# Four graph attention layers: the casts of the adjacency split between ScalarE and GpSimd

## The chip, the cores and the metric

The kernel runs on 1 core of one Trainium2 chip. The metric is the device time of one execution in microseconds (us), lower is better. The program has five instruction streams: TensorE (PE in the profile), VectorE (DVE), ScalarE (ACT), GpSimd (POOL) and SyncE (SP, which here only issues DMAs). They meet through semaphores.

## What is computed

Four pre-norm residual layers on a graph of N = 2048 nodes with 128 features: h = relu(layernorm(x)), x = x + attention_layer(h). Every layer uses the same adjacency matrix of 2048 x 2048 int32 zeros and ones. Cut to what matters:

```python
e = leaky_relu(s1[:, None] + s2[None, :], 0.2)      # scores from two vectors
att = softmax(where(adj > 0, e, NEG), axis=-1)      # 2048 x 2048
hp = elu(att @ Wh)                                  # layers 0, 2, 3; gelu in layer 1
# layer 0 does this for 8 heads, joins them and multiplies by W_out
```

The kernel factors exp(leaky_relu(s1 + s2)) into a row factor, a column factor and a maximum, so that an unnormalized probability is max(rho[i], t[j]) * adjT[j, i], with the column factor folded into V. The adjacency is needed as a bf16 factor of 0 or 1.

## The kernel before

**Tiling.** The transposed adjacency is cut into 32 tiles of 128 x 1024: tile n has half c = n // 16 of the columns (output rows) and block j = n % 16 of the neighbours. All stay in SBUF as bf16 (adjT) for the rest of the program. A head of layer 0 is two units of 16 steps, one for each half c; unit u = 2h + c. Step j of a unit: VectorE makes one tile of probs from rho, t_now and adjT (line 703), and TensorE multiplies it with V[j] in eight accumulating products that the trace shows as 16 matmuls (line 317). Between them lies a ring of 8 probs tiles, so VectorE is at most 8 steps ahead. In the first pass over the tiles (units 0 and 1, head 0) VectorE also waits for tile n of adjT to be cast.

**The loading of the adjacency.** SyncE issues 32 DMAs of 512 KB (line 181) into a staging buffer with STAGE = 5 slots, in order of n; DMA n waits for the cast of tile n - 5. ScalarE casts each tile with one activation, Sign (line 430), in groups that stand between its other duties: tiles 0 to 5 before the exponentials (line 549), then three after each of four groups of V (line 555), tiles 18 to 23 after copy_mean (line 558), and tiles 24 to 31 after it has copied waL (line 562). copy_mean waits for mean_rows, which TensorE does after step 7 of unit 0 (line 383); the copy of waL waits for later_vectors after step 13 (line 384).

**The row of rho.** rho is one row for each head, computed for all 8 heads in rho_rows. For unit 0 it is spread by TensorE. Otherwise GpSimd sends it through DRAM: for each half c it waits for the exponentials (rho_ready), stores the half of rho_rows to rho_dram (line 210), waits until that has landed, and, for c = 1, loads it spread over 128 partitions into rho (load_rho, line 205). Unit 1 waits for this load at its step 0 (line 789). The loads of the later heads follow in a loop (line 214), each after the unit that reads the old half.

**The end of a unit.** The work that follows a unit is done inside the next one (head0_asides, line 750): after step 7 VectorE computes the denominators (line 709), after step 8 it divides (line 725), for which ScalarE must first have made fill (lines 511 to 516, after the denominators), after step 10 it does the elu and a block transpose (lines 735 to 740); ScalarE then moves 16 blocks into hpT (line 529). TensorE takes hpT after its own step 10 of that unit (OUT_AT, line 341), and VectorE adds the result after its step 15.

ScalarE runs its stream in order, so fill_rows of unit 0 comes behind the cast of tile 31:

```python
            cast(24, 2 * NT)
            with act.Fori(0, H - 1) as h:
                finish(2 * h, 0)
```

Of the kernel before, what the change touches and what calls it, by code (L numbers as in the profile page):

```python
# [14 lines left out]
def gat_stack(nc, x, adj_t, w0, w0_t, a0, w_out, b_out, w1_t, w1, r1, w2, w2_t, av2, w3, w3_t, av3, out):  # L15
# [3 lines left out]
    ALU, ACT, AX = mybir.AluOpType, mybir.ActivationFunctionType, mybir.AxisListType  # L19
# [4 lines left out]
    NT = N // P  # L24
    CH = N // 2
# [5 lines left out]
    STAGE = 5  # L31
# [12 lines left out]
    with ctx:  # L44
        def sb(name, shape, dt=fp32):
            return ctx.enter_context(nc.sbuf_tensor(name, shape, dt))

        def sem(name):
            return ctx.enter_context(nc.semaphore(name))

        adjT = sb("adjT", [P, NT, N], bf16)
        stage = sb("stage", [P, STAGE, CH], i32)
# [55 lines left out]
        adj_in = [sem(f"adj_in{s}") for s in range(STAGE)]  # L108
        ident_zero = sem("ident_zero")
        ident_ready = sem("ident_ready")  # L110
        adj_ready = sem("adj_ready")
        wa_ready = sem("wa_ready")
        dve_step = sem("dve_step")
        wa_psum = sem("wa_psum")
# [46 lines left out]
        def group(c, k):  # L161

            return acc[:, c, k // PER_BANK, (k % PER_BANK) * VW:(k % PER_BANK) * VW + VW]

        def first_norm(n):

            return isinstance(n, int) and n == 0

        @block.sync
        def _(sp):  # L170
            for c in range(2):
                sp.dma_start(X[:, c * NK:(c + 1) * NK, :], x_v[:, c * NK:(c + 1) * NK, :]).then_inc(x_in[c], 16)
            sp.dma_start(W0t[:, :, :], w0_t.rearrange("h d f -> d h f")).then_inc(w0t_in, 16)
            sp.dma_start(a0_sb[:, :, :], a0).then_inc(w0t_in, 16)
            sp.dma_start(W0[:, :, :], w0.rearrange("h f d -> f h d")).then_inc(w0_in, 16)

            for n in range(2 * NT):
                c, j = n // NT, n % NT
                if n >= STAGE:
                    sp.wait_ge(adj_ready, n - STAGE + 1)  # L180
                sp.dma_start(stage[:, n % STAGE, :], adj_t[j * P:(j + 1) * P, c * CH:(c + 1) * CH]).then_inc(adj_in[n % STAGE], 16)
            sp.wait_ge(x_written, 10)
            sp.dma_start(out_v[:, 0:NK, :], X[:, 0:NK, :]).then_inc(out_done, 16)
            sp.wait_ge(x_written, 12)
            sp.dma_start(out_v[:, NK:NT, :], X[:, NK:NT, :]).then_inc(out_done, 16)
            sp.wait_ge(out_done, 32)

        @block.gpsimd
        def _(pool):
            nc.gpsimd.memset(ident[:, :], 0.0).then_inc(ident_zero, 1)  # L190
            pool.wait_ge(ident_zero, 1)
            nc.gpsimd.affine_select(out=ident[:, :], in_=ident[:, :], compare_op=ALU.not_equal, fill=1.0,  # L192
                                    base=0, pattern=[[-1, P]], channel_multiplier=1).then_inc(ident_ready, 1)
            for l, w in enumerate((w1_t, w2, w3)):
                pool.dma_start(WL[:, l, 0:D], w).then_inc(w_in, 16)
            for l, w in enumerate((w1, w2_t, w3_t)):
                pool.dma_start(WLt[:, l, :], w).then_inc(w_in, 16)
            for l, a in enumerate((r1, av2, av3)):
                pool.dma_start(aL_sb[:, l, :], a).then_inc(w_in, 16)
            pool.dma_start(bias_rep[:, :], b_out.rearrange("(o d) -> o d", o=1).to_broadcast([P, D])).then_inc(w_in, 16)  # L200
            pool.dma_start(Wout[:, :, :], w_out.rearrange("(h d) o -> d h o", h=H)).then_inc(w_in, 16)


            def load_rho(h, c):
                pool.dma_start(rho[:, c * CH:(c + 1) * CH],
                               rho_dram[bass.ds(h, 1), c * CH:(c + 1) * CH].to_broadcast([P, CH])).then_inc(rho_in[c], 16)

            for c in range(2):
                pool.wait_ge(rho_ready, 2 * c + 2)
                pool.dma_start(rho_dram[:, c * CH:(c + 1) * CH], rho_rows[:, c * CH:(c + 1) * CH]).then_inc(rho_stored, 16)  # L210
                pool.wait_ge(rho_stored, 16 * c + 16)
                if c == 1:
                    load_rho(0, c)
            with pool.Fori(0, H - 1) as h:
                for c in range(2):
                    pool.wait_ge(probs_ready, h * (2 * NT) + (c + 1) * NT)
                    load_rho(h + 1, c)

        @block.tensor
        def _(pe):  # L220
            def transpose_normed(n, c):

                for r in range(2 * c, 2 * c + 2):
                    pe.wait_ge(norm_act if r % 2 else norm_dve, 2 * n + c + 1)
                    for k in range(4):
                        last = nc.tensor.transpose(side[:, r % 2, k * P:(k + 1) * P],  # L226
                                                   xn[:, (r % 2) * 4 + k, :], ident[:, :])
                    last.then_inc(hT_psum, 1)
                if first_norm(n) or c == 1:
                    keep_warm(WARM_SHORT, idle_first if first_norm(n) else idle)  # L230
                pe.wait_ge(hT_ready, n * 4 + 2 * c + 2)
                if c == 0:
                    pe.wait_ge(wa_ready, n + 1)
# [190 lines left out]
        def _(act):  # L424
            def cast(n0, n1):

                for n in range(n0, n1):
                    c, j = n // NT, n % NT
                    act.wait_ge(adj_in[n % STAGE], 16 * (n // STAGE + 1))
                    nc.scalar.activation(adjT[:, j, c * CH:(c + 1) * CH], stage[:, n % STAGE, :], ACT.Sign).then_inc(adj_ready, 1)  # L430

            def relu_transposed(n, c):
                act.wait_ge(rstd_ready, n + 1 if first_norm(n) else 2 * n + c)
                for k in range(4, NK):
                    at = c * NK + k
                    last = nc.scalar.activation(xn[:, k, :], X[:, at, :], ACT.Identity, bias=nwt[:, 3, at:at + 1],  # L436
                                                scale=nwt[:, 0, at:at + 1])
                last.then_inc(norm_act, 1)
                for r in range(2 * c, 2 * c + 2):
                    act.wait_ge(hT_psum, n * 4 + r + 1)  # L440
                    nc.scalar.activation(hT[:, r * 512:(r + 1) * 512], side[:, r % 2, :], ACT.Relu,  # L441
                                         accum_out=hsum[:, r:r + 1]).then_inc(hT_ready, 1)
# [104 lines left out]
            relu_transposed(0, 0)  # L547
            relu_transposed(0, 1)
            cast(0, 6)
            factors(0, H)  # L550
            rho_exp(0, 0, H)
            act.wait_ge(tv_ready, 2)
            nc.scalar.activation(v_now[:, :], v_all[:, 0, :], ACT.Copy).then_inc(tv_ready, 1)
            act.wait_ge(tv_ready, 3)
            scale_v(0, lambda g: (cast(6 + 3 * g, 9 + 3 * g), g == 1 and rho_exp(0, 1, H)))
            copy_mean(1, H)
            take_mean(mean_w[:, 0:D], 1)
            cast(18, 24)
            act.wait_ge(waL_psum, 1)
            nc.scalar.activation(WL[:, 0:3, D], side[:, 0, 1:6:2], ACT.Copy)  # L560
# [43 lines left out]
        def _(dve):  # L604
# [181 lines left out]
            def rho_and_adj(h, c, blocks):  # L786
                def before(j):
                    if j == 0 and c == 1:
                        dve.wait_ge(rho_in[1], (h + 1) * 16)
                    elif j == 0 and not isinstance(h, int):  # L790
                        dve.wait_ge(rho_in[0], h * 16)
                    if blocks:
                        dve.wait_ge(adj_ready, c * NT + j + 1)
                return before

            def add_bias():
# [25 lines left out]
            for _, work in head0_asides(2 * H - 1, 1, store=False):  # L822
                work()
# [29 lines left out]
            with dve.Fori(0, 2) as l:  # L853
                base[0] = l * PER + outside
                n, u, f = l + 2, 2 * l + U2, 2 * l + 2 * H
# [50 lines left out]
```

## Time and profile before

| what | us |
|---|---|
| median of 3 runs (lowest to highest) | 807.01 (806.09 to 807.22) |
| the profiled execution | 807.67 |
| its span in the trace | 805.6 |
| TensorE busy | 775.1 (96%) |
| VectorE busy | 636.6 (79%) |
| ScalarE busy | 320.5 (40%) |
| GpSimd busy | 16.1 (2%) |
| casts of the adjacency on ScalarE, 32 | 31.7 |

The trace counts from the start of the span; the profiled execution has 2.1 us around it. The granted clock is the share of full speed that TensorE was given in a stretch.

### The profile page before, as it was taken

Reading aid. Unit: us, or ns where it says so; the run is one execution under the profiler, and the core shown is the slowest. Engines: PE = TensorE matmul, PEld = TensorE weight load, DVE = VectorE, ACT = ScalarE, POOL = GpSimd, SP = SyncE. Lnnn points to the kernel's source line nnn. Section 1 sums busy time; section 2 is a strip of 40 time slices with the busy share of each in tenths; the row PEclk is TensorE's granted clock in tenths of the full one; section 3 lists DMA queues with packets and bytes.
Section 4 is the critical chain, followed back from the end, with each engine's and each line's share of the span. In section 5 each row is a group of like instructions: output and inputs, shape, how many; then the busy total and the mean of one; then the engine's idle time right before and its main releaser. Section 6 shows DMA issues by size and latency. Waiting matters only on the chain. (4 is left out here: it accounts for less than half of the span.)

```text
span 805.6 us, 16634 instructions
## 1 busy us (share of the span) xinstructions
PE 775.1 (96%) x6666; PEld 755.5 (94%) x6666; DVE 636.6 (79%) x1084; ACT 320.5 (40%) x847; POOL 16.1 (2%) x34
## 2 busy tenths in 40 slices
PE   8999799999999999999999999999899989998995
PEld 8699799999999999999999999998799979987995
DVE  4595787877967978888788788796599569966994
ACT  2866443543345146144244354345420262135212
POOL 3000000000000000000000000000000000000000
PEclk8899999999999999999999999999999999999999
DMA  9687000000000000000000000000000000000000
GB/s 284 209 294 259 27 2 27 3 23 26 0 26 26 0 26 0 26 26 0 26 26 0 26 12 14 0 1 1 1 2 1 2 1 1 2 0 0 0 26 26
DMA packets 13708, 29.24 MB, mean 36 GB/s; under 512 B 1264, under 2 KB 7408, under 8 KB 13680
## 3 DMA queue, kind: packets, MB, share of 16 engines
q1 hardware_dynamic: 10992, 19.93, 7.5%
q0 software_dynamic: 2688, 8.92, 3.1%
q8 instruction: 20, 0.33, 0.2%
q14 instruction: 8, 0.07, 0.0%
HBM read 27.73 MB, written 1.11 MB: 36 GB/s over the span
## 5 line engine op out<-in xcount | busy, mean ns | idle before, releaser
L317 PE MATMUL acc<-V,probs 128*128 128x129 f32 x5632 | 639.0, 275 | 5.3 <-DVE probs L703 5.3
L317 PEld LDWEIGHTS acc<-V,probs 128*128 128x128 f32 x5632 | 634.0, 192 | 9.4 <-DVE probs L703 4.9
L703 DVE SCALAR_TENSOR_TENSOR probs<-rho,t_now,adjT 128x1024 f32<-128x1024 f32 x352 | 430.5, 1278 | 32.0 <-PE acc L317 26.2
L529 ACT ACTIVATE hpT<-rows 32x256 f32<-32x256 f32 x240 | 99.4, 414 | 76.2 <-DVE rows L740 73.5
L514 ACT ACTIVATE fill<-mean_now,empty 128x128 f32<-128x128 f32 x160 | 48.9, 394 | 102.4 <-DVE den L716 102.3
L748 DVE TENSOR_TENSOR X<-X,side 128x512 f32<-128x512 f32 x32 | 22.0, 688 | 61.5 <-PE side L341 61.5
L521 ACT ACTIVATE rows<-rows 128x512 f32<-128x512 f32 x44 | 27.7, 630 | 73.2 <-DVE rows L725 48.2
L725 DVE SCALAR_TENSOR_TENSOR rows<-acc,den,fill 128x128 f32<-128x128 f32 x160 | 43.9, 342 | 6.2 <-ACT fill L514 5.5
L463 ACT ACTIVATE V<-v_now 128x4 f32<-128x4 f32 x32 | 6.7, 209 | 85.8 <-PE side L262 85.8
L341 PE MATMUL side<-Wout,hpT 128*128 (+1 forms) x256 | 33.0, 284 | 4.5 <-ACT hpT L529 4.2
L436 ACT ACTIVATE xn<-X,nwt 128x128 f32<-128x128 f32 x36 | 14.8, 483 | 56.3 <-DVE nwt L640 56.3
L465 ACT ACTIVATE V<-side,v_now 128x128 f32<-128x128 f32 x128 | 36.1, 365 | 0.0
L341 PEld LDWEIGHTS side<-Wout,hpT 128*128 128x128 f32 x256 | 31.4, 200 | 4.9 <-issue 4.4
L262 PE MATMUL side<-W,hT 128*128 (+1 forms) x256 | 34.7, 279 | 0.0
L282 PEld LDWEIGHTS acc<-ident 128*128 128x128 f32 x236 | 31.1, 215 | 3.5 <-ACT V L479 1.9
L282 PE MATMUL acc<-ident 128*128 128x128 f32 x236 | 32.3, 300 | 1.8 <-POOL ident L192 1.6
L262 PEld LDWEIGHTS side<-W,hT 128*128 128x128 f32 x256 | 31.8, 195 | 2.4 <-issue 2.4
L430 ACT ACTIVATE adjT<-stage 128x1024 bf16<-128x1024 int32 x32 | 31.7, 1058 | 4.7 <-DMA stage<-in_adj_t_dram 4.7
L441 ACT ACTIVATE hT<-side 128x512 f32<-128x512 f32 x18 | 10.6, 594 | 26.7 <-PE side L226 26.6
L653 DVE COPY den<-acc 128x6 f32<-128x6 f32 x22 | 3.5, 157 | 21.9 <-PE acc L317 21.9
L736 DVE SCALAR_TENSOR_TENSOR rows<-rows 128x1024 f32<-128x1024 f32 x16 | 19.6, 1225 | 0.6
L740 DVE STREAM_TRANSPOSE rows<-rows 128x1024 f32<-128x1024 f32 x15 | 18.7, 1246 | 0.5
(107 smaller groups left out, 277.8 us busy)
## 6 DMA issues: line engine op xcount, KB each, us to landing
stage<-in_adj_t_dram SPq DMA_DIRECT2D x32, 512.0 KB, 6.6
rho<-rho_dram POOLq DMA_DIRECT2D x15, 512.0 KB, 3.9
X<-in_x_dram SPq DMA_DIRECT2D x2, 512.0 KB, 4.4
out_dram<-X SPq DMA_DIRECT2D x2, 512.0 KB, 3.2
W0t<-in_W_t_dram SPq DMA_DIRECT2D x1, 512.0 KB, 7.1
W<-in_L_gnn_W_heads_dram SPq DMA_DIRECT2D x1, 512.0 KB, 7.7
Wout<-in_L_gnn_W_out_dram POOLq DMA_DIRECT2D x1, 512.0 KB, 10.4
WL<-in_L_gnn_W_dram POOLq DMA_DIRECT2D x2, 64.0 KB, 5.9
```

What stands on the lines that cost most here:

```text
L262: last = nc.tensor.matmul(side[:, g % 2, k * D:(k + 1) * D], hT[:, j * P:(j + 1) * P], w, start=True, stop=True)
L282: nc.tensor.matmul(where, ident[:, :], ident[:, :], start=True, stop=True)
L317: last = nc.tensor.matmul(group(c, k), probs[:, j % RING, k * P:(k + 1) * P], V[:, j, :], start=(j == 0 and k % PER_BANK == 0), stop=(j == ...
L341: last = nc.tensor.matmul(side[:, b, k * D:(k + 1) * D], hpT[:, 4 * b + k, :], w, start=True, stop=True)
L430: nc.scalar.activation(adjT[:, j, c * CH:(c + 1) * CH], stage[:, n % STAGE, :], ACT.Sign).then_inc(adj_ready, 1)
L465: last = nc.scalar.activation(V[:, 4 * g + k, 0:D], side[:, g % 2, k * D:(k + 1) * D], ACT.Copy, scale=v_now[:, 4 * g + k:4 * g + k + 1])
L514: ins = nc.scalar.activation(fill[:, k, :], mean_now[:, :], ACT.Copy, scale=empty[:, c, k:k + 1])
L521: nc.scalar.activation(rows[:, 1, 4 * b:4 * b + 4, :], rows[:, 0, 4 * b:4 * b + 4, :], func).then_inc(act_ready, 1)
L529: last = nc.scalar.activation(hpT[b:b + Q, :, a:a + Q], rows[a:a + Q, 1, :, b:b + Q], ACT.Copy)
L703: nc.vector.scalar_tensor_tensor(probs[:, j % RING, :], rho[:, c * CH:(c + 1) * CH], t_now[:, j:j + 1], adjT[:, j, c * CH:(c + 1) * CH], A ...
L725: ins = nc.vector.scalar_tensor_tensor(rows[:, 0, k, :], group(c, k)[:, 0:D], den[:, 3, k:k + 1], fill[:, k, :], ALU.mult, ALU.add)
L748: nc.vector.tensor_tensor(at, at, side[:, b, :].rearrange("p (k d) -> p k d", k=4), ALU.add).then_inc(x_added, 1)
```

## The change

Tiles with n % 3 == 2 (2, 5, 8, ..., 29: ten of the 32) are cast by GpSimd with a comparison, is_gt against 0, and the other 22 by ScalarE as before. The one semaphore that counted casts becomes two, and a helper, wait_adj, turns the number of a tile into the semaphore and the count to wait for; SyncE and VectorE use it. In GpSimd's stream tiles 2, 5, 8 and 11 stand ahead of the store of the first half of rho_rows, tiles 14, 17, 20 and 23 ahead of the store of the second half (and so ahead of load_rho for unit 1), and tiles 26 and 29 behind that load and ahead of the loop.

```diff
-        adj_ready = sem("adj_ready")
+        adj_act = sem("adj_act")
+        adj_pool = sem("adj_pool")
...
+        def on_pool(n):
+
+            return n % 3 == 2
+
+        def wait_adj(engine, n):
+
+            before = sum(on_pool(i) for i in range(n + 1))
+            engine.wait_ge(adj_pool if on_pool(n) else adj_act, before if on_pool(n) else n + 1 - before)
...
                 if n >= STAGE:
-                    sp.wait_ge(adj_ready, n - STAGE + 1)
+                    wait_adj(sp, n - STAGE)
...
+            def cast(n0, n1):
+
+                for n in range(n0, n1):
+                    c, j = n // NT, n % NT
+                    if on_pool(n):
+                        pool.wait_ge(adj_in[n % STAGE], 16 * (n // STAGE + 1))
+                        nc.gpsimd.tensor_scalar(adjT[:, j, c * CH:(c + 1) * CH], stage[:, n % STAGE, :], 0, None,
+                                                ALU.is_gt).then_inc(adj_pool, 1)
+
             for c in range(2):
+                cast(12 * c, 12 * c + 12)
                 pool.wait_ge(rho_ready, 2 * c + 2)
                 pool.dma_start(rho_dram[:, c * CH:(c + 1) * CH], rho_rows[:, c * CH:(c + 1) * CH]).then_inc(rho_stored, 16)
                 pool.wait_ge(rho_stored, 16 * c + 16)
                 if c == 1:
                     load_rho(0, c)
+            cast(24, 2 * NT)
...
-                    act.wait_ge(adj_in[n % STAGE], 16 * (n // STAGE + 1))
-                    nc.scalar.activation(adjT[:, j, c * CH:(c + 1) * CH], stage[:, n % STAGE, :], ACT.Sign).then_inc(adj_ready, 1)
+                    if not on_pool(n):
+                        act.wait_ge(adj_in[n % STAGE], 16 * (n // STAGE + 1))
+                        nc.scalar.activation(adjT[:, j, c * CH:(c + 1) * CH], stage[:, n % STAGE, :], ACT.Sign).then_inc(adj_act, 1)
...
                     if blocks:
-                        dve.wait_ge(adj_ready, c * NT + j + 1)
+                        wait_adj(dve, c * NT + j)
```

## Rows read from the trace of the kernel before

**Rows 1.** The page, part 1: busy us (share of the span) and instructions.

```profile
PE 775.1 (96%) x6666; PEld 755.5 (94%) x6666; DVE 636.6 (79%) x1084; ACT 320.5 (40%) x847; POOL 16.1 (2%) x34
```

**Rows 2.** Waits of TensorE, 60 to 560 us: total, times, longest.

```profile
PE side L341 <- ACT hpT L529: 4.2, 1, 4.2
PE acc L246 <- ACT hT L441: 0.9, 1, 0.9
```

**Rows 3.** Timeline of ScalarE: start, us, line, operation, tiles, count, [idle before, releaser].

```profile
56.46 1.09 ACT L502 ACTIVATE mean_w<-side 128x512 f32<-128x512 f32 x2 [4.79 <-PE side L302]
57.92 4.84 ACT L430 ACTIVATE adjT<-stage 128x1024 bf16<-128x1024 int32 x5
...
67.87 4.84 ACT L430 ACTIVATE adjT<-stage 128x1024 bf16<-128x1024 int32 x5
...
76.84 1.06 ACT L430 ACTIVATE adjT<-stage 128x1024 bf16<-128x1024 int32 x1 [2.61 <-DMA stage<-in_adj_t_dram]
78.08 1.06 ACT L430 ACTIVATE adjT<-stage 128x1024 bf16<-128x1024 int32 x1 [0.19 <-DMA stage<-in_adj_t_dram]
79.04 2.43 ACT L514 ACTIVATE fill<-mean_now,empty 128x128 f32<-128x128 f32 x8
...
88.19 6.80 ACT L529 ACTIVATE hpT<-rows 32x256 f32<-32x256 f32 x16 [4.90 <-DVE rows L740]
```

**Rows 4.** Timeline of VectorE: steps of units 0 and 1, denominators, division.

```profile
49.61 8.46 DVE L703 SCALAR_TENSOR_TENSOR probs<-rho,t_now,adjT 128x1024 f32<-128x1024 f32 x7
58.25 1.28 DVE L703 SCALAR_TENSOR_TENSOR probs<-rho,t_now,adjT 128x1024 f32<-128x1024 f32 x1 [0.18 <-PE acc L317]
60.04 1.28 DVE L703 SCALAR_TENSOR_TENSOR probs<-rho,t_now,adjT 128x1024 f32<-128x1024 f32 x1 [0.50 <-PE acc L317]
...
72.70 0.15 DVE L653 COPY den<-acc 128x6 f32<-128x6 f32 x1
...
73.23 0.20 DVE L716 RECIPROCAL den<-den 128x8 f32<-128x8 f32 x1
...
80.34 2.29 DVE L725 SCALAR_TENSOR_TENSOR rows<-acc,den,fill 128x128 f32<-128x128 f32 x8 [5.50 <-ACT fill L514]
...
86.91 1.25 DVE L740 STREAM_TRANSPOSE rows<-rows 128x1024 f32<-128x1024 f32 x1
```

**Rows 5.** Timeline of TensorE: the first output projection.

```profile
95.24 3.61 PE L341 MATMUL side<-Wout,hpT 128*128 x16 [4.20 <-ACT hpT L529]
```

**Rows 6.** Busy us of each engine by stretch, TensorE's granted clock, DMA share, GB/s.

```profile
34.00:58.00 24.00, 23.60 (x175) 20.72 (x174) 23.48 (x23) 17.01 (x33) 1.08 (x2) 0.94 0.92 318
95.20:98.80 3.60, 3.56 (x17) 3.56 (x18) 0.69 (x1) 0.04 (x1) 0.10 (x1) 0.53 0.44 146
```

**Rows 7.** Timeline of SyncE's queue, 58 to 62 us.

```profile
59.01 3.17 SPq L181 DMA_DIRECT2D stage<-in_adj_t_dram  x4
```

**Rows 8.** Timeline of GpSimd: its two elementwise instructions, then rho's store and load.

```profile
0.87 0.20 POOL L190 MEMSET ident<- 128x128 f32 x1 [0.29 <-POOLq L896]
1.30 0.28 POOL L192 TENSOR_SCALAR_AFFINE_SELECT ident<-ident 128x128 f32<-128x128 f32 x1 [0.23 <-POOL ident L190]
...
42.23 0.51 POOL L210 DMA_DIRECT2D rho_dram<-rho_rows  x1 [9.46 <-ACT rho_rows L456]
47.45 0.57 POOL L205 DMA_DIRECT2D rho<-rho_dram  x1 [4.70 <-DMA rho_dram<-rho_rows]
```

**Rows 9.** DMA issues at 24.6, 59.0, 47.4, 58.8 and 94.8 us: size, us to landing.

```profile
stage<-in_adj_t_dram SPq DMA_DIRECT2D x1, 512.0 KB, 3.6
...
stage<-in_adj_t_dram SPq DMA_DIRECT2D x1, 512.0 KB, 4.9
...
rho<-rho_dram POOLq DMA_DIRECT2D x1, 512.0 KB, 9.1
...
rho<-rho_dram POOLq DMA_DIRECT2D x1, 512.0 KB, 5.0
...
rho<-rho_dram POOLq DMA_DIRECT2D x1, 512.0 KB, 4.0
```

## The prediction

> **What bounds the kernel now.** The page's busy shares come first: TensorE is busy for 775.1 us of a span of 805.6 [rows 1]. ScalarE, which the change relieves, is busy for 40%, so fewer casts are worth something only where TensorE waits for ScalarE. So I read TensorE's waits next, over the stretch that holds the casts and the seven heads after them. From 60 to 560 us it waits twice for ScalarE: 4.2 us for hpT, and 0.9 us in the next layer [rows 2]. The 4.2 us end at 95.24 [rows 5], and the weights matter: everything after that runs on TensorE without a gap to the next layer, so whatever moves 95.24 moves the end by the same amount. The matmuls behind that wait run at a granted clock of 0.53, about the lower level of 1.2 GHz against 2.4 [rows 6]; the 16 matmuls take 3.61 us [rows 5].
>
> The timelines of ScalarE and VectorE show where the 4.2 us come from. Unit 0's denominators are there at 73.23 + 0.20 = 73.43 [rows 4], but ScalarE casts to the end of tile 31, 78.08 + 1.06, and begins fill at 79.04; it had stood 2.61 us for the DMA of tile 30 [rows 3]. VectorE waits 5.50 us for fill [rows 4]. From the start of fill the chain is fixed: 79.04, division at 80.34, steps 9 and 10, elu, transpose to 86.91 + 1.25, the 16 block moves to 88.19 + 6.80 = 94.99 [rows 3, 4]. That is **15.95 us from fill to hpT**, and TensorE goes on 0.25 later. So the number that decides is the time at which fill of unit 0 can start.
>
> **What the change removes.** Ten casts of 0.97 us (4.84 us for five [rows 3]) leave ScalarE, 9.7 us of busy time. Up to 58 us TensorE is busy 23.60 us of 24 [rows 6] and VectorE has made all 16 probs tiles of unit 0 at 49.61 + 8.46 = 58.07 while TensorE ends that unit more than 13 us later (it paces the ring at 60.04 - 58.25 = 1.79 us a step [rows 4], and 95.24 less the wait of 4.20 less 11 steps of unit 1 is 71.35). So earlier casts there are worth nothing. At the end ScalarE gets tiles 24 to 31 done a little sooner, but it is not short of ScalarE time there: it waits for DMAs 30 and 31 [rows 3], and these wait for the casts of 25 and 26, which cannot start before 67.87. By itself this would let fill start between 77 and 79 instead of 79.04, a gain of 0 to 2 us.
>
> **What the change moves.** The program of GpSimd now has four casts ahead of each store of rho. The first store loses its place from 32 us to about 40, with no one behind it before the load for unit 2, which is asked for after 58 us. The second is another matter. Before, the store went at 42.23 and the load at 47.45 [rows 8], and the load landed 9.1 us later [rows 9], at 56.5, just ahead of VectorE's step 0 of unit 1 at 58.25 [rows 4]. Now both stand behind the cast of tile 23. The earliest time for that follows from the code and rows: slot 23 % 5 is free when tile 18 is cast; tile 18 remains ScalarE's, and stands behind copy_mean, which waits for TensorE's step 7. So it is cast from 57.92 [rows 3], and the DMA of tile 23 goes at 59.01 [rows 7], after the change as before it. No engine that the change relieves is on this path. From there:
>
> - DMA of tile 23: 3.6 us with little beside it, 4.9 beside a load of rho [rows 9]. That load of rho now comes later, so I take 3.8: 62.8.
> - The cast on GpSimd. No row shows one. GpSimd's nearest instruction that reads a tile is the affine select, 0.28 us for 128 columns; eight times that is 2.3. Its memset of 128 columns took 0.20 [rows 8]; ScalarE's cast 0.97 stands for the low end, as I have no reason to think GpSimd quicker. I take 1.6, between them: 64.4. A gain below nothing is excluded, since a cast takes some time and none stood there.
> - Store to load: 47.45 - 42.23 = 5.2 us [rows 8], at a busy DMA, as here: 69.7 with a hand-over.
> - The load: 4.0 us alone, 5.0 beside two stage loads, 9.1 behind a row of them [rows 9]. At 69.7 the DMAs of tiles 29 and 30 have just been issued (casts of 24 and 25 from 67.87), so I take 5.3: **rho for unit 1 at 75.0**.
>
> VectorE stands at step 0 of unit 1 from 58.07 to 75.0; behind that wait are queued all probs tiles of unit 1, the denominators, the division and the elu. TensorE runs dry at 71.35 and starts again about 1.3 us after rho, at 76.3, an idle time of 4.9 us. That stall itself has cover: the 11 steps before hpT then end at 76.3 + 19.7 = 96.0, or 97.8 with a slow start of 1.8, and TensorE has to wait for hpT anyway (below: to 101.6).
>
> What counts is the chain on VectorE. Steps 0 to 7 of unit 1 had been made long before 72.70; now they come after 75.0, at 8.46 / 7 = 1.21 us each [rows 4], so 9.7 us, then the denominators, 73.43 - 72.70 = 0.7 us. Fill starts at 75.0 + 10.4 = 85.4 instead of 79.04, 6.4 us later; ScalarE has been free since about 78. The 15.95 us follow as before, hpT is there at 101.4, and TensorE resumes 6.4 us later, at 101.6. Its wait there is 3.8 to 5.6 us, near the 4.2 of before, so I leave the slow clock behind it as it is: 3.61 us for 16 matmuls against 1.79 for 16 at full clock, 1.8 us in both.
>
> The other waits are small. Tiles 26 and 29 are cast behind the load of rho; DMA 31 waits for tile 26 and lands at about 77, needed by VectorE not before 90. The load for unit 2 goes after the cast of tile 29, about 76, and is needed at 106. The two counters cost no instruction on a busy engine.
>
> **Sum.** 6.4 us on the profiled execution's 807.67 is 814.1; the median of the runs is 0.66 below that execution, so I forecast 813.5. Low end of the mechanism: 59.01 + 3.6 + 1.0 + 5.1 + 4.0 = 72.7, fill 4.1 us later, 811.1. If TensorE kept the full clock behind its wait, 1.8 less, 809.3. High end: 59.01 + 4.9 + 2.3 + 5.3 + 9.1 = 80.6, 12 us later, 819.
>
> **Rivals.** *Rho is no later than unit 1 needs it (the other side).* The point from which this decides: fill starts earlier than 79.04 only when rho lands before 79.04 - 10.4 = 68.6. Then what is left is ScalarE's gain of 0 to 2 us, 805 to 807. For it speaks that the load had 1.7 us of room before, and that TensorE has 13 us of probs in its ring when VectorE ends unit 0; against it, that the three fixed pieces alone (DMA 3.6, store 5.1, load 4.0, from 59.01) give 71.7 with a cast that costs nothing. It needs one of them at half of what any row shows.
>
> *GpSimd and VectorE hold each other up.* In 34 to 58 us VectorE is busy 23.48 us of 24 [rows 6], nearly all in line 703, which reads rho and adjT. No row shows GpSimd reading a tile at that time. If GpSimd gets through only when VectorE stands still, tile 11 is cast when VectorE itself waits for it, about 52 us; store 1 behind it takes 5.2, tile 14 is cast to 60, tile 17 to 62, DMA 19 waits for tile 14 and DMA 23 stands behind four others (five of 512 KB at 318 GB/s, 8 us): landing at 69 to 70, rho at 82, fill 13 us later, 820. If they only take turns, each cast costs VectorE up to 2.3 us where it is 8 tiles ahead, which is free, and tile 23 is cast while VectorE stands: the main forecast. The Trainium skill ("SBUF — State Buffer", section "Who interferes with whom") states that a VectorE instruction with two SBUF inputs and a GpSimd instruction that reads SBUF exclude each other and the second to issue waits for the whole of the first; by it 813.5 stands if the turns alternate and about 820 if VectorE always comes first, and no row of before shows which.
>
> The same notes ("GPSIMD Engine Reference", section "Performance versus the Vector engine") give 1.8 cycles per element at 1.2 GHz for a tight loop of one input, so an estimate of 1.5 us for 1024 columns; the sum by it would be 0.1 us lower.
>
> *A cast on GpSimd is much dearer than any row suggests*, say 4 us for a comparison with two conversions. Tiles 11, 14, 17, 20 still keep up (about 16 us apart in all, over 39 to 59), and the forecast moves by 2.4 to 816.
>
> **Chances.** Main chain with the bounds above 0.76; mutual hold-up 0.09; dear cast 0.08; rho in time after all 0.07, of which 0.04 faster and 0.03 within 0.2%. A difference of 0.2%, 1.6 us, is about what a measurement of this kernel can tell from none. Faster 0.04, same 0.03, slower 0.93. The range from 810.0 to 819.5 leaves out the rival on the other side, the worst of the hold-up and the tail of both ends.
>
> **What would show it.** In the trace of the changed kernel: the DMA of tile 23 still at about 59.0; GpSimd's cast of tile 23 at 62 to 64 and its length; store and load of rho 5.2 us apart; a new wait of VectorE's line 703 for rho of some 17 us, ending near 75; TensorE idle from 71 to 76; fill near 85.4, released by the denominators and no longer by a cast; TensorE's output projection at about 101.6 instead of 95.24, and from there all work shifted alike. The prediction is wrong if the load of rho lands before 68.6, if fill does not follow the load by 10.4 us, or if VectorE waits for a tile cast by GpSimd in unit 0.

## The result and the profile after

The changed kernel takes 816.2 us (median of 4 runs, 815.76 to 821.01) against 806.55 us (median of 4, 805.96 to 807.22). The ratio is 1.0133, with a 95% interval of 1.0094 to 1.0172: slower, by 8 to 14 us. The two profiled executions are 816.23 and 807.67 us, 8.56 apart, and their spans 814.2 and 805.6, 8.6 apart. TensorE's busy time is the same (775.0 us, before 775.1); what is new is idle time between 60 and 104 us. ScalarE's share fell from 40% to 38%, GpSimd's rose from 2% to 6%.

First GpSimd's timeline of the changed kernel (start, us, line, operation, tiles, count, [idle before, releaser]): the casts of tiles 14 and 17, of 20, of 23, then the store of rho's second half and the load for unit 1.

```profile
48.98 7.57 POOL L224 TENSOR_SCALAR adjT<-stage 128x1024 bf16<-128x1024 int32 x2 [4.93 <-DMA rho_dram<-rho_rows]
60.32 2.99 POOL L224 TENSOR_SCALAR adjT<-stage 128x1024 bf16<-128x1024 int32 x1 [3.77 <-DMA stage<-in_adj_t_dram]
64.95 2.77 POOL L224 TENSOR_SCALAR adjT<-stage 128x1024 bf16<-128x1024 int32 x1 [1.64 <-DMA stage<-in_adj_t_dram]
67.66 0.60 POOL L230 DMA_DIRECT2D rho_dram<-rho_rows  x1
72.98 0.56 POOL L215 DMA_DIRECT2D rho<-rho_dram  x1 [4.72 <-DMA rho_dram<-rho_rows]
```

Where the load went out at 47.45 before [rows 8], it goes at 72.98. The DMAs on that path: SyncE's issue of tile 23, its time to landing, and that of rho's load.

```profile
59.27 0.33 SPq L191 DMA_DIRECT2D stage<-in_adj_t_dram  x1
...
stage<-in_adj_t_dram SPq DMA_DIRECT2D x1, 512.0 KB, 5.6
...
rho<-rho_dram POOLq DMA_DIRECT2D x1, 512.0 KB, 4.2
```

VectorE's timeline answers [rows 4]: the last seven steps of unit 0, the first eight of unit 1 behind a wait of 16.67 us for rho, the denominators.

```profile
50.79 9.90 DVE L725 SCALAR_TENSOR_TENSOR probs<-rho,t_now,adjT 128x1024 f32<-128x1024 f32 x7
77.35 9.65 DVE L725 SCALAR_TENSOR_TENSOR probs<-rho,t_now,adjT 128x1024 f32<-128x1024 f32 x8 [16.67 <-DMA rho<-rho_dram]
86.92 0.16 DVE L675 COPY den<-acc 128x6 f32<-128x6 f32 x1
...
87.46 0.20 DVE L738 RECIPROCAL den<-den 128x8 f32<-128x8 f32 x1
```

ScalarE's timeline answers [rows 3]: it has finished tile 31 at 81.16 and then waits 6.54 us for the denominators, so fill has changed its releaser, from the casts to VectorE.

```profile
58.18 2.01 ACT L452 ACTIVATE adjT<-stage 128x1024 bf16<-128x1024 int32 x2
...
80.10 1.06 ACT L452 ACTIVATE adjT<-stage 128x1024 bf16<-128x1024 int32 x1 [3.51 <-DMA stage<-in_adj_t_dram]
87.70 2.45 ACT L536 ACTIVATE fill<-mean_now,empty 128x128 f32<-128x128 f32 x8 [6.54 <-DVE den L738]
...
96.87 6.80 ACT L551 ACTIVATE hpT<-rows 32x256 f32<-32x256 f32 x16 [4.90 <-DVE rows L762]
```

TensorE's timeline: it runs dry for 7.04 us, then has 11 steps, then waits 3.25 us for hpT. It resumes at 103.92, where it resumed at 95.24 before [rows 5]: 8.68 later, which is the whole difference.

```profile
67.83 3.82 PE L338 MATMUL acc<-V,probs 128*128 128x129 f32 x32
78.69 21.98 PE L338 MATMUL acc<-V,probs 128*128 128x129 f32 x176 [7.04 <-DVE probs L725]
103.92 3.46 PE L362 MATMUL side<-Wout,hpT 128*128 x16 [3.25 <-ACT hpT L551]
```

### The profile page after: what moved, and what is told of

Same layout as the page of the kernel before. It is cut to its first block and busy times, and to the rows that moved or that the text cites. A ratio compares the mean times of both kernels' runs of the same rounds, so it can differ in the third digit from the quotient of the medians.

```text
span 814.2 us, 16634 instructions
## 1 busy us (share of the span) xinstructions
PE 775.0 (95%) x6666; PEld 755.6 (93%) x6666; DVE 639.4 (79%) x1084; ACT 311.6 (38%) x837; POOL 47.2 (6%) x44
## 5 line engine op out<-in xcount | busy, mean ns | idle before, releaser
L725 DVE SCALAR_TENSOR_TENSOR probs<-rho,t_now,adjT 128x1024 f32<-128x1024 f32 x352 | 432.2, 1285 | 44.2 <-PE acc L338 22.2
L362 PE MATMUL side<-Wout,hpT 128*128 (+1 forms) x256 | 32.8, 284 | 3.5 <-ACT hpT L551 3.2
L224 POOL TENSOR_SCALAR adjT<-stage 128x1024 bf16<-128x1024 int32 x10 | 31.1, 3119 | 33.5 <-DMA stage<-in_adj_t_dram 28.5
L215 POOL DMA_DIRECT2D rho<-rho_dram x15 | 8.1, 537 | 408.5 <-DVE probs L725 403.7
L452 ACT ACTIVATE adjT<-stage 128x1024 bf16<-128x1024 int32 x22 | 22.4, 1058 | 9.8 <-DMA stage<-in_adj_t_dram 9.7
```

The lines of the kernel that those rows point to most:

```text
L224: nc.gpsimd.tensor_scalar(adjT[:, j, c * CH:(c + 1) * CH], stage[:, n % STAGE, :], 0, None, ALU.is_gt).then_inc(adj_pool, 1)
L362: last = nc.tensor.matmul(side[:, b, k * D:(k + 1) * D], hpT[:, 4 * b + k, :], w, start=True, stop=True)
L725: nc.vector.scalar_tensor_tensor(probs[:, j % RING, :], rho[:, c * CH:(c + 1) * CH], t_now[:, j:j + 1], adjT[:, j, c * CH:(c + 1) * CH], A ...
```

## The experiments

The start of the program, to unit 0, varies by several us from run to run (single runs of the kernel before lay between 804.4 and 811.4 in the experiments). From TensorE's return, the start of the first output projection, to the end of the span it is 710.2 to 711.6 us in the traces of this table, and 708.9 in e5 and e7, so differences of about 1 us arise behind it too. So each trace is also read from a fixed event in it: the start of copy_mean on ScalarE. "Behind" is the span less that start; the last column is its difference from before.

| kernel | copy_mean | fill | span | behind | against before |
|---|---|---|---|---|---|
| before | 56.46 | 79.04 | 805.6 | 749.1 | |
| changed | 56.72 | 87.70 | 814.2 | 757.5 | +8.3 |
| e1_place_only | 54.48 | 86.88 | 813.6 | 759.1 | +10.0 |
| e11_place_only_hold | 54.44 | 86.80 | 814.3 | 759.9 | +10.7 |
| e3_tile23_act | 59.22 | 85.84 | 813.3 | 754.1 | +4.9 |
| e4_tiles20_23_act | 56.52 | 83.16 | 810.2 | 753.7 | +4.5 |
| e8_place_early | 57.13 | 78.72 | 805.4 | 748.3 | -0.9 |
| e2_load_first | 61.37 | 82.95 | 809.4 | 748.0 | -1.1 |
| e6_load_first_act26 | 57.17 | 78.88 | 806.7 | 749.5 | +0.4 |
| e5_before_act26 | 55.68 | 75.32 | 800.4 | 744.7 | -4.4 |
| e7_before_act28 | 55.11 | 74.50 | 799.6 | 744.5 | -4.7 |

### e1_place_only: the place of rho's store and load alone

On the kernel before; no cast on GpSimd.

```diff
             for c in range(2):
+                if c == 1:
+                    pool.wait_ge(adj_ready, 24)
                 pool.wait_ge(rho_ready, 2 * c + 2)
```

> The kernel before with all 32 casts on ScalarE; GpSimd only waits for the cast of tile 23 before it stores the second half of rho_rows. My theory (the place of rho's store and load is the whole cost): ScalarE ends tile 23 at about 65.0, load issued at 70.3 (5.3 us after the store, as in the changed kernel), VectorE's step 0 of unit 1 at 74.7, fill 10.35 us later at 85.0 instead of 79.04, so 6.0 us slower than before. The rest of the change's 8.7 us would be the longer cast on GpSimd and the later landing of tile 23. Rival (the slow casts on GpSimd, or their contention with VectorE, are the cost): within 0.5 us of before.

Measured: 817.51 us against 807.7, ratio 1.014 (1.0092 to 1.0187). The place alone costs as much as the whole change, which settles the cause; the size was missed by 4 us (6.0 expected, 9.8 by the medians, 10.0 behind copy_mean). GpSimd's and VectorE's timelines of this kernel:

```profile
62.29 0.51 POOL L212 DMA_DIRECT2D rho_dram<-rho_rows  x1 [30.89 <-ACT adjT L432]
68.35 0.57 POOL L205 DMA_DIRECT2D rho<-rho_dram  x1 [5.54 <-DMA rho_dram<-rho_rows]
...
76.54 9.66 DVE L705 SCALAR_TENSOR_TENSOR probs<-rho,t_now,adjT 128x1024 f32<-128x1024 f32 x8 [20.32 <-DMA rho<-rho_dram]
```

Store to load took 6.1 us (5.3 in the changed kernel), load to use 8.2 (4.4 there). So without GpSimd's casts the store went out earlier, and store and load were slower.

### e11_place_only_hold: what made that load slow

On e1_place_only.

```diff
+            pool.wait_ge(adj_ready, 2 * NT)
             with pool.Fori(0, H - 1) as h:
```

> The run with only the place of rho's store and load moved, in which the load for unit 1 took 8.1 us to be used where the changed kernel took 4.4; here the load for unit 2 is held back until all 32 tiles are cast, so that it does not follow 0.8 us behind the load for unit 1. Theory A (the second load delayed the first): step 0 of unit 1 comes 4.5 to 5.5 us after the load's issue, 3 us earlier, and the time falls to about 6.5 to 7.5 us above before. Theory B (the stage DMAs in flight delayed it): still about 8 us from issue to use, and about 9.5 us above before.

Measured: 816.96 against 807.82, ratio 1.0116 (1.008 to 1.0152). GpSimd's and VectorE's timelines:

```profile
68.56 0.57 POOL L205 DMA_DIRECT2D rho<-rho_dram  x1 [5.80 <-DMA rho_dram<-rho_rows]
...
76.46 9.66 DVE L706 SCALAR_TENSOR_TENSOR probs<-rho,t_now,adjT 128x1024 f32<-128x1024 f32 x8 [20.28 <-DMA rho<-rho_dram]
```

Still 7.9 us from issue to use: theory A falls. What is left is the stage DMAs beside it. The stretch from the load's issue to its use, first here, then in the changed kernel, where it took 4.4 (columns: us, busy PE, PEld, DVE, ACT, POOL, granted clock, DMA share, GB/s):

```profile
68.56:76.40 7.84, 0.80 (x8) 0.61 (x6) 0.00 (x0) 3.92 (x5) 0.57 (x1) 0.84 0.85 274
72.98:77.30 4.32, 0.00 (x0) 0.00 (x0) 0.00 (x0) 2.11 (x2) 4.29 (x3) 0.87 0.60 231
```

In e4_tiles20_23_act the share is 1.00 and the load takes 7.8 us. So a busier DMA goes with a slower load, but the stage DMAs were not switched off by themselves: that they are the cause is not shown.

### e3_tile23_act and e4_tiles20_23_act: how far the store must move

On the changed kernel; the second has `and n not in (20, 23)`.

```diff
-            return n % 3 == 2
+            return n % 3 == 2 and n != 23
```

> The changed kernel with tile 23 given back to ScalarE, GpSimd's other nine stay. My theory: the store follows the cast of tile 20, which ended at 63.3 in the changed kernel, instead of tile 23's at 67.7; load issued at 68.6, VectorE's step 0 at 73.0, fill at 83.4: 4.4 us less than the changed kernel, 4.3 us more than before. Rival: if the cost were the casts themselves, one of ten gives back 0.9 us.

Measured: 813.35 against 807.7, ratio 1.0069 (1.0045 to 1.0093). GpSimd, VectorE and TensorE:

```profile
62.45 0.60 POOL L230 DMA_DIRECT2D rho_dram<-rho_rows  x1
67.70 0.56 POOL L215 DMA_DIRECT2D rho<-rho_dram  x1 [4.65 <-DMA rho_dram<-rho_rows]
...
74.72 10.43 DVE L725 SCALAR_TENSOR_TENSOR probs<-rho,t_now,adjT 128x1024 f32<-128x1024 f32 x8 [11.67 <-DMA rho<-rho_dram]
...
102.06 3.78 PE L362 MATMUL side<-Wout,hpT 128*128 x16 [4.44 <-ACT hpT L551]
```

From copy_mean to TensorE's return is 42.8 us, against 38.8 before and 47.2 in the changed kernel: one cast of ten, moved off the path of rho, gives back half, as expected, and not the tenth of the loss (0.9 us) that the rival gives. That it gives back just the 4.4 us forecast is partly luck. The store came 7.7 us earlier against copy_mean than in the changed kernel (copy_mean itself was 2.5 us later), and 3.4 us of that was lost again: the load took 7.0 us to its use instead of 4.4, and the eight steps 10.43 instead of 9.65.

> The changed kernel with tiles 20 and 23 given back to ScalarE. My theory: the store follows the cast of tile 17 at 56.6, load issued at 61.9, rho there at 66.3, which is before the 68.6 from which it decides: fill is bound by ScalarE's last casts at 77 to 79, so -2 to 0 us against before, though VectorE still waits some 7 us for rho. Rival (any wait of VectorE for rho costs its own length): 7 us slower than before; rival (the casts cost): 7 us slower as well.

Measured: 810.8 against 807.7, ratio 1.0034 (1.0014 to 1.0054): slower by 3 us where no loss was expected. GpSimd, VectorE and ScalarE:

```profile
56.30 0.60 POOL L230 DMA_DIRECT2D rho_dram<-rho_rows  x1
63.24 0.56 POOL L215 DMA_DIRECT2D rho<-rho_dram  x1 [6.35 <-DMA rho_dram<-rho_rows]
71.21 2.77 POOL L224 TENSOR_SCALAR adjT<-stage 128x1024 bf16<-128x1024 int32 x1 [7.41 <-DMA stage<-in_adj_t_dram]
75.06 3.28 POOL L224 TENSOR_SCALAR adjT<-stage 128x1024 bf16<-128x1024 int32 x1 [1.08 <-DMA stage<-in_adj_t_dram]
...
71.17 11.30 DVE L725 SCALAR_TENSOR_TENSOR probs<-rho,t_now,adjT 128x1024 f32<-128x1024 f32 x8 [10.69 <-DMA rho<-rho_dram]
...
83.16 2.45 ACT L536 ACTIVATE fill<-mean_now,empty 128x128 f32<-128x128 f32 x8 [4.29 <-DVE den L738]
```

The mechanism holds and two durations did not: store to load 6.9 us, load to use 7.9, so rho came at 71.2 and not at 66.3, 2.6 behind the point of 68.6; and VectorE's eight steps took 11.30 us instead of 9.7, since GpSimd's casts of tiles 26 and 29 fell beside them. 2.6 + 1.6 = 4.2 is fill's delay (83.16 against 79.04: 4.1). The rival of 7 us is out as well: 10.7 us of waiting for rho cost 4.

### e8_place_early: a wait for rho that lands in time

On the kernel before, as e1_place_only, with `pool.wait_ge(adj_ready, 16)`.

> The kernel before with the store of rho's second half held only until the cast of tile 15 (ScalarE ends it at about 51.7). Theory (only a load that lands after the point of 68.6 costs anything): store 52, load 57.3 to 58.5, landed at 62 to 66; VectorE waits 3 to 8 us for rho at step 0 of unit 1, TensorE does not run dry, and the time is that of before within 0.5 us. Rival (each us that VectorE waits for rho costs one): 3 to 8 us slower.

Measured: 807.52 against 806.9, ratio 1.0004 (0.9987 to 1.0021). A wait of VectorE, and TensorE's return:

```profile
DVE probs L705 <- DMA rho<-rho_dram: 2.6, 1, 2.6
...
94.92 3.06 PE L343 MATMUL side<-Wout,hpT 128*128 x16 [3.21 <-ACT hpT L531]
```

Rho's load was issued at 56.27 and VectorE began unit 1 at 61.3. VectorE waits 2.6 us, a little less than expected, TensorE does not run dry, and the time is that of before. So it is the point, not the wait, that decides.

### e2_load_first: all of the change but the place

On the changed kernel.

```diff
+            cast(0, 12)
             for c in range(2):
-                cast(12 * c, 12 * c + 12)
                 pool.wait_ge(rho_ready, 2 * c + 2)
                 pool.dma_start(rho_dram[...], rho_rows[...]).then_inc(rho_stored, 16)
-                pool.wait_ge(rho_stored, 16 * c + 16)
-                if c == 1:
-                    load_rho(0, c)
-            cast(24, 2 * NT)
+            pool.wait_ge(rho_stored, 32)
+            load_rho(0, 1)
+            cast(12, 2 * NT)
```

> The changed kernel with all ten casts on GpSimd, but both stores of rho_rows and the load for unit 1 stand behind tile 11 and ahead of tile 14. My theory: load issued at about 49.5, landed before 58.7, no wait of VectorE for rho; fill is again bound by ScalarE's last casts, which wait for DMAs 30 and 31, at 77.5 to 79.5, so -1.5 to +0.5 us against before. Rival (GpSimd's casts of 2.8 us and up are too slow for the staging buffer, or hold VectorE up): still 4 us or more slower than before, with VectorE or ScalarE waiting for tiles.

Measured: 808.53 against 807.7, ratio 1.0014 (0.9994 to 1.0034). GpSimd's load, ScalarE's fill, TensorE's return:

```profile
50.82 0.56 POOL L215 DMA_DIRECT2D rho<-rho_dram  x1 [3.43 <-DMA rho_dram<-rho_rows]
...
82.95 2.43 ACT L535 ACTIVATE fill<-mean_now,empty 128x128 f32<-128x128 f32 x8
...
99.17 3.43 PE L361 MATMUL side<-Wout,hpT 128*128 x16 [3.22 <-ACT hpT L550]
```

With ten casts on GpSimd and rho early, the loss is gone, and hardly anything is gained: fill is 21.6 us behind copy_mean (22.6 before), right behind ScalarE's last cast, as before. The start of the program took longer in this trace (copy_mean at 61.37); more on it below.

### e5_before_act26, e7_before_act28, e6_load_first_act26: what the casts were really bound by

e5 on the kernel before (e7 with 28 in place of 26; e6 is e5's edit on e2_load_first).

```diff
-            cast(18, 24)
+            cast(18, 26)
             act.wait_ge(waL_psum, 1)
...
-            cast(24, 2 * NT)
+            cast(26, 2 * NT)
```

> The kernel before with ScalarE's casts of tiles 24 and 25 moved ahead of the copy of waL, where it stood idle for 2.7 us; nothing on GpSimd. Theory (the 4.2 us wait of TensorE for hpT comes from casts that wait for DMAs 30 and 31, and these for the casts of 25 and 26): DMAs 29 and 30 go about 2 us earlier, fill starts at 76 to 77.5 instead of 79.04, 1.5 to 3 us faster than before. Rival (the DMA rate bounds the last tiles whatever the order): within 0.5 us of before.

Measured: 803.22 against 806.9, ratio 0.9957 (0.9934 to 0.9979). ScalarE's cast of tile 24 and fill; TensorE's return, and the stretch behind it (us, busy PE, PEld, DVE, ACT, POOL, granted clock, DMA share, GB/s):

```profile
65.13 1.06 ACT L430 ACTIVATE adjT<-stage 128x1024 bf16<-128x1024 int32 x1 [1.75 <-DMA stage<-in_adj_t_dram]
...
75.32 2.43 ACT L514 ACTIVATE fill<-mean_now,empty 128x128 f32<-128x128 f32 x8
...
91.53 2.05 PE L341 MATMUL side<-Wout,hpT 128*128 x16 [1.27 <-ACT hpT L529]
...
91.50:93.60 2.10, 2.07 (x18) 2.08 (x19) 0.69 (x1) 0.02 (x1) 0.09 (x1) 1.00 0.54 209
```

By the medians 3.7 us (the interval gives 1.7 to 5.3), more than expected, for two reasons: fill comes 2.9 us nearer to copy_mean, and behind the wait, now 1.27 us instead of 4.20, the clock is granted in full (1.00, against 0.53 [rows 6]), so the 16 matmuls take 2.05 us instead of 3.61 [rows 5].

> As the run with tiles 24 and 25 moved ahead, but with 24 to 27: the copy of waL comes at about 69, still ahead of unit 1 on TensorE at 71.4. Theory: DMA 31 goes 1 to 2 us earlier too; fill starts at 75 to 76.5, 3 to 4 us faster than before, and up to 6 if TensorE no longer waits and keeps its clock. Risk: if tile 27 lands late, the copy of waL is late and TensorE waits ahead of unit 1. Rival (DMA rate): within 0.5 us of before.

Measured: 802.94 against 806.9, ratio 0.9945 (0.9923 to 0.9967), not apart from e5. ScalarE and TensorE:

```profile
74.50 2.43 ACT L514 ACTIVATE fill<-mean_now,empty 128x128 f32<-128x128 f32 x8
...
90.70 2.05 PE L341 MATMUL side<-Wout,hpT 128*128 x16 [0.89 <-ACT hpT L529]
```

Only 0.89 us of the wait is left. This is the lowest median of all, with every cast on ScalarE.

> GpSimd casts its ten tiles, rho's stores and load stand ahead of tile 14, and ScalarE casts tiles 24 and 25 ahead of waL. Theory: DMAs 29 to 31 are now tied to GpSimd's casts of 23 and 26, each 2.8 to 3.9 us; fill relative to copy_mean no better than with the casts on ScalarE alone: 0 to 2.5 us faster than before, and behind the same order without GpSimd. If GpSimd's casts helped, it would be the faster of the two.

Measured: 807.71 against 806.9, ratio 1.0006 (0.9987 to 1.0025). GpSimd's cast of tile 26, and fill:

```profile
70.75 3.51 POOL L224 TENSOR_SCALAR adjT<-stage 128x1024 bf16<-128x1024 int32 x1 [3.63 <-DMA stage<-in_adj_t_dram]
...
78.88 2.43 ACT L535 ACTIVATE fill<-mean_now,empty 128x128 f32<-128x128 f32 x8
```

The gain of e5 is lost when GpSimd casts its share: tile 26 is done at 74.3, and DMA 31 waits for it. In e5 ScalarE had it done at 69.1. Of these 5.2 us, 1.5 come from the later start of this trace (copy_mean at 57.17, in e5 55.68).

### e9_gpsimd_reads and e10_gpsimd_writes: do the two engines hold each other up

On the kernel before, behind the load of rho for unit 1; e10 has `nc.gpsimd.memset(dum_in[:, :], 0)` in the loop. The scratch tiles, their semaphore and a first memset of dum_in at the start of GpSimd's program come with it and are not shown.

```diff
+            for k in range(8):
+                pool.wait_ge(dum, k + 1)
+                nc.gpsimd.tensor_scalar(dum_out[:, :], dum_in[:, :], 0, None, ALU.is_gt).then_inc(dum, 1)
             with pool.Fori(0, H - 1) as h:
```

> The kernel before with eight casts of a scratch tile (128 x 1024, int32 to bf16, the instruction of the change) on GpSimd behind the load of rho for unit 1, at 48 to 80 us, that nobody waits for. Theory (GpSimd's reads and VectorE's line 703 exclude each other in turns): a cast takes 3.6 to 3.9 us beside VectorE against 2.8 alone, and a step of line 703 that meets one takes longer than 1.21 us, 7 steps 9.3 to 9.9 instead of 8.5; no time lost, as VectorE is ahead there. Rival (no exclusion; the long casts have another reason): steps at 1.21 us as in the kernel before.

> The same with eight memsets of 128 x 1024 in place of the casts: GpSimd writes and reads nothing. Theory (it is GpSimd's read that collides with VectorE's two operands): steps of line 703 at 1.21 us, the memsets equally long beside VectorE and alone. Rival (any work of GpSimd collides): steps lengthened as with the casts.

One run of each: 806.23 and 803.06 us, beside one of 804.47 for before, which says nothing on time. GpSimd's eight instructions and VectorE's steps beside them, first e9_gpsimd_reads:

```profile
46.24 26.01 POOL L220 TENSOR_SCALAR dum_out<-dum_in 128x1024 bf16<-128x1024 int32 x8
...
47.46 24.14 DVE L710 SCALAR_TENSOR_TENSOR probs<-rho,t_now,adjT 128x1024 f32<-128x1024 f32 x15
```

and e10_gpsimd_writes:

```profile
44.50 8.04 POOL L220 MEMSET dum_in<- 128x1024 int32 x8
...
45.45 9.79 DVE L710 SCALAR_TENSOR_TENSOR probs<-rho,t_now,adjT 128x1024 f32<-128x1024 f32 x8
```

Beside the casts a step takes 24.14 / 15 = 1.61 us and a cast 3.25; beside the memsets a step takes 1.22, as alone, and a memset 1.0. So GpSimd's writes alone do not lengthen the steps, and the read is what is left; the cast also converts and compares, which no run separates from it. The steps were lengthened more than expected, the casts less (median 3.09 us of one, the rest of the 3.25 is the hand-over between two).

## Why the prediction was right, and where its terms were off

The forecast of 813.5 us was in the right direction and for the right reason; the measured 816.2 lies in the range. Point by point:

- *What bounds the kernel:* held. TensorE's return from hpT moved by 8.68 us and the span by 8.6. From fill to hpT it is 103.67 - 87.70 = 15.97 us, forecast 15.95; from rho to fill 87.70 - 77.35 = 10.35, forecast 10.4.
- *Tile 18 stays behind copy_mean:* held; the DMA of tile 23 went at 59.27 (59.01 before), copy_mean being 0.26 later.
- *DMA of tile 23, taken at 3.8:* 5.7 to its cast at 64.95. The claim that little would be beside it failed. The cast of tile 14 ended only at 53.4, because GpSimd stood 4.93 us in the wait for the first store (which I had called a loss with no one behind it), and that cast took 4.41 us beside VectorE. So DMAs 19 to 22 went out between 53.4 and 56.9, where before the last of them had gone by 52.0, and 20 to 22 were still under way at 59.27. This alone is 1.9 us of the error.
- *The cast, taken at 1.6:* 2.77 alone, above my high end of 2.3; from its start to the store 2.71, so 1.1 us of error. The affine select, scaled by columns, was the nearer row, and the low end from ScalarE's cast had pulled the value down.
- *Store to load, 5.2 and 0.1 for the hand-over:* 5.3. *The load, 5.3:* 4.4 to its use, 0.9 to the good. Sum: 0.3 + 1.9 + 1.1 - 0.9 is 2.4, and rho came at 77.35 instead of 75.0. The last term is luck: it hides a part of the other two errors.
- *The stall of TensorE is covered:* held; it was dry for 7.04 us and still waited 3.25 us for hpT, though its 11 steps took 21.98 us and not the 19.7 to 21.5 of the forecast. The stretch behind had its slow clock, 3.46 us for 16 matmuls (3.61 before).
- *The point of 68.6:* held from both sides, though the runs only bracket it: rho at 61.3 costs nothing (e8), and at 71.2 the sum with 68.6 accounts for 2.6 of the 4.1 us (e4). The place alone makes the whole loss (e1).
- *What is removed is worth 0 to 2 us:* at most its low end. With rho early, ten casts less on ScalarE changed the trace by -1.1 us behind copy_mean and the time by +0.14%, with an interval from -0.06 to +0.34%: no gain is shown.
- *The rivals:* rho in time did not occur, and e2 shows what it would have given. The mutual hold-up was the mild form: unit 0's last seven steps took 9.90 us against 8.46 [rows 4], free there. It was not free in e4, beside unit 1. The dear cast came half of the way: 2.77 us, between the 1.6 taken and the rival's 4.

What I did not see is that two terms of the path go against each other. In place-only the store goes 5.4 us earlier (62.29 against 67.66), yet it costs no less, as store to load takes 6.1 us and the load 8.2 to its use. In the changed kernel the load stands beside less DMA work (share 0.60) and takes 4.4. Over eleven loads of nine of the kernels the share, with the load's own part in it, was 0.60 to 0.71 where they landed in 4.2 to 5.0 us, and 0.80 to 1.01 where they took 6.3 to 9.1. That GpSimd's slow casts spread the stage DMAs out and so made the load fast is likely, but not shown.

## What to carry to other kernels

Before you put work into an engine's idle time, list what else stands in that engine's program order: an engine that is 2% busy, as GpSimd here, may still carry one transfer with a deadline, and what counts is by when that transfer must land. Work back from the wait to be shortened to what releases it: here that was the order of casts around a copy on ScalarE, and moving two or four tiles' casts ahead of that copy gave 0.4 to 0.6%, where moving a third of the work cost 1.3%.

## What the runs showed of the hardware that was not expected

**GpSimd's cast is dear.** 128 x 1024, int32 to bf16 with a comparison: 2.77 us alone, 2.6 times ScalarE's 1.06, and up to 4.41 beside VectorE in the changed kernel; its memset of the same tile took 1.0. "GPSIMD Engine Reference" of the Trainium skill ("Performance versus the Vector engine") gives 1.8 cycles per element as the best case of a tight loop; 2.77 us is an estimated 3.2 cycles at that page's 1.2 GHz.

**The collision is partial.** In 26.0 us GpSimd made eight casts, which alone take 22.2 us, while VectorE in 24.1 us of them made 15 steps, which alone take 18.2 us. If each had excluded the other for whole instructions, the sum, 40 us, would have been needed. "SBUF — State Buffer" of the Trainium skill ("Who interferes with whom") calls the port that the two share an exclusive lock, and says that a VectorE instruction with two SBUF inputs contends with a GpSimd instruction that reads SBUF and not with one that only writes. The second agrees with the runs; a lock held for whole instructions does not. Each cast cost VectorE 6.0 / 8 = 0.75 us.

**A load of 512 KB on GpSimd's queue took 3.7 to 9.1 us to land:** 4.2 in the changed kernel, 7.8 in e4 and e11. It took longer where more DMAs were under way (the shares are given above).

**The start of unit 0 goes with the granted clock.** From the first reduction of layer 0 (cmax) to copy_mean it took 30.0 to 33.4 us. The granted clock in the stretch from 10 to 17 us behind cmax orders all thirteen traces: at 1.00 it took 30.0 to 30.1 us (the changed kernel, e1, e4, e5, e9, e10, e11), at 0.89 to 0.91 30.7 to 30.9 (before, e7, e8), at 0.56 to 0.64 32.8 to 33.4 (e2, e3, e6). Those three have adjacency casts on GpSimd, and so have the changed kernel and e4. The stretch 36 to 43 us, first in e3_tile23_act, then in e4_tiles20_23_act:

```profile
36.00:43.00 7.00, 6.81 (x21) 3.98 (x21) 5.15 (x5) 2.83 (x5) 6.49 (x3) 0.55 0.88 279
```

```profile
36.00:43.00 7.00, 6.56 (x45) 4.94 (x46) 7.00 (x7) 3.95 (x7) 6.39 (x2) 1.00 0.81 272
```

The granted clock was 0.55 in one and 1.00 in the other, with 21 matmuls against 45. If it is so in most runs, it would explain why e3 lost 5.7 us by the medians and 4.1 by the path of rho, and why e2 lies 0.8 us above before though its trace is shorter behind copy_mean. Whether GpSimd's casts bring the lower clock about, or whether it is chance in so few traces, stays open. That they hold VectorE's first steps up does not explain it by itself: four of them took 5.65 us (4.87 before) in e3, but also in the changed kernel and in e4.
